# Eight early dense groups in place of nine, with the ninth's first steps kept in DRAM during the experts

## The reference

```python
# A: state space block and dense FFN, in sequences of 512 tokens
u  = rmsnorm(xn, ssm_norm_w)
Bu = einsum('btd,nd->btn', u, B_w)            # 64 states
h_t = sigmoid(log_lambda) * h_(t-1) + Bu_t    # a scan along the 512 tokens
x1 = xn + einsum('btn,dn->btd', hs, C_w) + D_skip * u
z  = rmsnorm(x1, ffn_norm_w)
A  = x1 + (silu(z @ w1.T) * (z @ w3.T)) @ w2.T          # inner size 688
# M: mixture of 32 experts, 8 per token, and a shared expert
scores = sigmoid(xn @ gate_w.T)               # best 4 of 8 groups, then the best 8 experts
routed = sum over the 8 of weight * (silu(xn @ w_gate[e].T) * (xn @ w_up[e].T)) @ w_down[e].T
shared = (silu(xn @ sh_gate.T) * (xn @ sh_up.T)) @ sh_down.T
```

## Time and profile before

| | us |
|---|---|
| median of 3 runs | 1865.17 (1863.17 to 1865.59) |
| the profiled execution | 1864.31 |
| its span | 1862.4 |
| PE busy in it (matmuls) | 1764.0 (95%) |
| DVE busy | 949.2 (51%) |
| ACT busy | 627.5 (34%) |
| POOL busy | 1033.7 (56%) |

### The profile page before, as it was taken

How to read it: one execution, slowest core, us unless ns; L and a number is a source line. 1 busy time by engine, 2 the same in 40 slices (tenths; PEclk the granted TensorE clock), 3 DMA queues, 4 the chain that set the end, 5 groups by cost and what they waited for, 6 DMA issues and landing times.

```text
span 1862.4 us, 27141 instructions
## 1 busy us (share of the span) xinstructions
PE 1764.0 (95%) x8166; PEld 1323.1 (71%) x8168; DVE 949.2 (51%) x2464; ACT 627.5 (34%) x1349; POOL 1033.7 (56%) x1058
## 2 busy tenths in 40 slices
PE   5798899999989999999999999999999969999995
PEld 2455565666658888888888888888888846666653
DVE  6577556433314444444444555556556535555555
ACT  5621222222214444444444444444444322222220
POOL 0001777777777777771000665555556067777776
PEclk9898999999989999999999999999999979999997
DMA  6714333645478899986555898889898554333333
GB/s 208 248 45 136 135 128 142 216 157 221 151 280 275 290 289 292 287 287 205 172 176 170 257 281 268 272 267 276 265 277 265 180 163 117 113 114 103 103 105 105
DMA packets 262594, 374.29 MB, mean 201 GB/s; under 512 B 30916, under 2 KB 227640, under 8 KB 261688
## 3 DMA queue, kind: packets, MB, share of 16 engines
q1 hardware_dynamic: 212392, 227.51, 39.4%
q0 software_dynamic: 49920, 145.03, 23.4%
q10 hardware_dynamic: 144, 0.03, 0.0%
HBM read 189.47 MB, written 182.98 MB: 200 GB/s over the span
## 4 chain that ended last, share of the span: by engine, by line
PE 89%; DVE 6%; DMA 1%; issue 1%; ACT 1%; POOL 1%; SPq 1%; POOLq 0%; DVEq 0%; ACTq 0%
PE ps L1260 27%; PE ps L1178 19%; PE ps L1277 13%; PE ps L1195 11%; PE ps L1251 7%; PE ps L1270 3%; PE ps L1160 2%; PE ps L1131 2%; PE ps L1098 1%; PE ps L1147 1%; PE ps L1170 1%; DMA big<-in_x 1%; POOL xe L529 1%; PE ps L1091 1%; SPq L366 0%
## 5 line engine op out<-in xcount | busy, mean ns | idle before, releaser
L529 POOL DMA_INDIRECT xe<-results,slots x512 | 517.5, 1011 | 490.8 <-DMA results<-arena 232.8
L1260 PE MATMUL ps<-big,arena 128*128 x2304 | 546.4, 380 | 2.2 <-ACT arena L647 2.2
L1260 PEld LDWEIGHTS ps<-big,arena 128*128 128x128 f32 x2304 | 427.9, 190 | 73.5 <-issue 3.0
L1028 DVE SCALAR_TENSOR_TENSOR arena<-arena,ps 128x128 f32<-128x128 f32 x576 | 175.0, 344 | 467.3 <-ACT arena L652 393.6
L518 POOL DMA_INDIRECT sorted_rows<-big,slots x256 | 258.3, 1009 | 84.0 <-issue 77.8
L1277 PE MATMUL ps<-big,arena 128*128 x1152 | 296.2, 380 | 0.0
L518 POOL DMA_INDIRECT sorted_rows<-xe,slots x256 | 246.3, 962 | 78.1 <-issue 78.1
L1178 PE MATMUL ps<-arena,w 128*128 128x512 f32 x640 | 287.7, 592 | 0.0
L620 ACT ACTIVATE arena<-ps 128x512 f32<-128x512 f32 (+1 forms) x128 | 76.3, 596 | 544.4 <-PE ps L1178 500.5
L937 DVE TENSOR_TENSOR arena<-arena,ps 128x512 f32<-128x512 f32 (+1 forms) x128 | 88.0, 688 | 329.3 <-ACT arena L620 328.1
L652 ACT ACTIVATE arena<-ps 128x256 f32<-128x256 f32 x288 | 110.7, 384 | 390.9 <-PE ps L1260 390.9
(11 more groups left out here) (160 smaller groups left out, 1355.6 us busy)
## 6 DMA issues: line engine op xcount, KB each, us to landing
arena<-sorted_rows SPq DMA_DIRECT2D x288, 288.0 KB, 3.9
results<-arena SPq DMA_DIRECT2D x288, 256.0 KB, 3.8
big<-in_x SPq DMA_DIRECT2D x32, 512.0 KB, 4.3
sorted_rows<-big SPq DMA_DIRECT2D x2, 4608.0 KB, 23.8
xe<-results,slots POOLq DMA_INDIRECT x512
out<-xe SPq DMA_DIRECT2D x64, 128.0 KB, 2.5
sorted_rows<-big SPq DMA_DIRECT2D x48, 144.0 KB, 1.8
big<-in_wexp SPq DMA_DIRECT2D x1, 5632.0 KB, 20.1
```

The costliest lines, as they stand in the source:

```text
L529: pool.indirect_dma_start(out=gathered_at[i % RING][:, k, :], out_offset=None, in_=results[half], in_offset=bass.IndirectOffsetOnAxis(ap=s ...
L1028: last = nc.vector.scalar_tensor_tensor(eh[n % 2][:, s, :], eg[n % 2][:, s, :], rows[n % RING][:, s, ds(e + D, 1)], ps[:, 2 + n % 2, (2 * ...
L1260: last = mm(ps[:, 2 + n % 2, s * D:(s + 1) * D], rT[n % 2][:, (2 * s + c) * P:(2 * s + c + 1) * P], big[:, ds(at_w + 2 * c * INNER, 2 * IN ...
```

## The change

There are eight early groups, 0 to 7 (`FIRST` = 8), and eight late ones, 8 to 15. The first steps of group 8 are still made inside group 7, and what they leave is kept in DRAM while the experts use the arena: `xT` in `kept_xT`, `zT` in `kept_zT`, and the sum of x and x1 in the rows of `parts`. After the experts the three are loaded again, and group 8 starts from them; the separate first steps in front of the late groups are gone. x is loaded anew for groups 9 to 15 (the four input tiles for 9 to 12 at once). There are eight places for gathered tiles in half 1 (four of them in `big`, over the expert weights), and four as before in half 0. In the last group the four last tiles are combined ahead of the wait for the last down product, and the down products are then added from PSUM to each tile.

```diff
     UP_AT = 64
-    FIRST = 9
+    FIRST = HT // GT
     LATE = range(FIRST, GROUPS)
...
         xe = sb("xe", [P, HT * ROW])
         rows_of = [big[:, AT_ROWS:].rearrange("p (t w) -> p t w", w=ROW), xe[:, :].rearrange("p (t w) -> p t w", w=ROW)]
-        gathered_at = [xe[:, j * K * D:(j + 1) * K * D].rearrange("p (k d) -> p k d", d=D) for j in range(RING)]
+
+        DEEP = 2 * RING
+        gathered_at = [a.rearrange("p (k d) -> p k d", d=D) for a in
+                       [xe[:, j * K * D:(j + 1) * K * D] for j in range(RING)]
+                       + [big[:, AT_ROWS + j * K * D:AT_ROWS + (j + 1) * K * D] for j in range(DEEP - RING)]]
+
+        def place(i):
+
+            return i % RING if i < HT else i % DEEP
+
+        def turn(i):
+
+            return i // RING if i < HT else (i - HT) // DEEP + (HT // RING if i % DEEP < RING else 0)
         part_tile = [xe[:, (RING * K + j) * D:(RING * K + j + 1) * D] for j in range(RING)]
...
             for g in range(FIRST - 1):
-                if g + 4 < FIRST:
+                if g + 4 <= FIRST:
                     sp.wait_ge(x_used, g + 1)
                     load_x(g + 4, g + 4)
...
                     load_wexp(0, AT_X)
             sp.wait_ge(x_used, FIRST)
-            load_wexp(AT_X, AT_ROWS)
             sp.wait_ge(xposed, FIRST)
             for j in range(4):
                 sp.wait_ge(scattered[0][j], 16 * K * QUARTER)
                 load_wexp(AT_ROWS + j * QUARTER * ROW, AT_ROWS + (j + 1) * QUARTER * ROW)
-            store_part(FIRST - 1)
+            sp.wait_ge(xT_ready, FIRST + 1)
+            sp.dma_start(kept_xT, xT.rearrange("p c n -> p (c n)")).then_inc(xT_stored, 16)
+            sp.wait_ge(x_used, FIRST + 1)
+            load_wexp(AT_X, AT_ROWS)
+            sp.dma_start(group_rows(parts, FIRST), part_early[FIRST % 2]).then_inc(part_kept, 16)
 
 
             def load_rows(n):
...
                 sp.wait_ge(summed, i + 1)
-                sp.dma_start(out[i * P:(i + 1) * P, :], gathered_at[i % RING][:, 0, :]).then_inc(out_stored[i % RING], 16)
-
-            sp.wait_ge(zposed, FIRST)
-            sp.wait_ge(gu_ready, CH * (FIRST - 1) + 2)
-            sp.wait_ge(rms_z_ready, FIRST)
+                sp.dma_start(out[i * P:(i + 1) * P, :], gathered_at[place(i)][:, 0, :]).then_inc(out_stored[place(i)], 16)
+
+            sp.wait_ge(xT_stored, 16)
+            sp.wait_ge(y_ready, FIRST + 1)
+            sp.wait_ge(z_ready, FIRST + 1)
             for n in range(RING):
                 load_rows(n)
+            sp.wait_ge(zT_ready, FIRST + 1)
+            sp.dma_start(kept_zT, zT.rearrange("p c n -> p (c n)")).then_inc(zT_stored, 16)
+            store_part(FIRST - 1)
             for par in range(2):
                 sp.wait_ge(part_stored[par], 16 * len(range(par, FIRST, 2)))
             for m in range(ALL + 2):
@@ -451,6 +478,8 @@
                         scattered_all(sp, 1)
                     if m + RING < ALL:
                         load_rows(m + RING)
+                    if m == ALL - 3:
+                        sp.dma_start(xT.rearrange("p c n -> p (c n)"), kept_xT).then_inc(xT_reloaded, 16)
                 n = m - 2
                 if n < 0:
...
             assert not summed_after(ALL - 2) and not summed_after(ALL - 1)
 
-            for g in range(FIRST, FIRST + 4):
+            for q in range(2):
+                sp.wait_ge(ey_stored[q], 16 * (ALL // RING))
+            sp.wait_ge(zT_stored, 16)
+            sp.dma_start(zT.rearrange("p c n -> p (c n)"), kept_zT).then_inc(zT_reloaded, 16)
+            for g in range(FIRST + 1, FIRST + 5):
                 load_x(g, g)
-            for i in range(HT, HT + GT):
-                load_part(i)
+            sp.wait_ge(part_kept, 16)
+            sp.dma_start(part_of(FIRST), group_rows(parts, FIRST)).then_inc(part_reloaded, 16)
             for g in LATE:
                 for t in range(GT):
-                    store_out((g - 1) * GT + t)
-                    if t == 2 and g + 4 < GROUPS:
-                        sp.wait_ge(x_used, g + 1)
-                        load_x(g + 4, g + 4)
+                    if g > FIRST:
+                        store_out((g - 1) * GT + t)
+                    if t == 2 and g + 5 < GROUPS:
+                        sp.wait_ge(x_used, g + 2)
+                        load_x(g + 5, g + 5)
             for t in range(GT):
                 store_out((GROUPS - 1) * GT + t)
-            for q in range(RING):
-                sp.wait_ge(out_stored[q], 16 * (NT // RING))
+            for i in range(NT - DEEP, NT):
+                sp.wait_ge(out_stored[place(i)], 16 * (turn(i) + 1))
 
 
...
+                    if turn(i):
+                        pool.wait_ge(out_stored[place(i)], 16 * turn(i))
                     for k in range(K):
                         pool.indirect_dma_start(
-                            out=gathered_at[i % RING][:, k, :], out_offset=None, in_=results[half],
+                            out=gathered_at[place(i)][:, k, :], out_offset=None, in_=results[half],
                             in_offset=bass.IndirectOffsetOnAxis(ap=slots[:, i, k:k + 1], axis=0)
-                        ).then_inc(gathered[i % RING], 16)
+                        ).then_inc(gathered[place(i)], 16)
 
 
         @block.scalar
...
             for g in range(FIRST):
-                act_group(g, g + 1 < FIRST)
+                act_group(g, True)
 
...
 
                 act.wait_ge(ey_ready, n + 1)
+                if n == 0:
+                    act.wait_ge(zT_stored, 16)
                 if n >= RING:
                     act.wait_ge(ey_stored[n % RING], 16 * (n // RING))
...
             e_out(ALL - 1)
 
-            act.wait_ge(ey_dve, ALL)
-            xT_copy(FIRST)
-            results_stored(act, ALL)
-            rms_z(FIRST)
-            zT_copy(FIRST)
             for g in LATE:
                 act_group(g, g + 1 < GROUPS)
...
                 dve.wait_ge(x_loaded[n % 4], 16 * ((GROUPS + n) // 4 + 1))
-                if 2 <= n < FIRST:
+                if 2 <= n <= FIRST:
                     dve.wait_ge(part_stored[n % 2], 16 * (n // 2))
-                tt(part_of(n), x_of(n), x1, ALU.add).then_inc(x_used, 1)
+                tt(part_early[n % 2] if n == FIRST else part_of(n), x_of(n), x1, ALU.add).then_inc(x_used, 1)
 
             def make_z(n):
...
             def finish_part(g):
                 dve.wait_ge(down_done, CH * (g + 1))
+                if g == FIRST:
+                    dve.wait_ge(part_reloaded, 16)
                 for b in range(2):
                     last = tt(part_of(g)[:, 2 * b:2 * b + 2, :], part_of(g)[:, 2 * b:2 * b + 2, :],
...
                     dve.wait_ge(part_loaded[i % RING], 16 * (i // RING + 1))
                     rest = part_tile[i % RING]
-                tt(y[:, 0, :], y[:, 0, :], rest, ALU.add).then_inc(summed, 1)
+                last = tt(y[:, 0, :], y[:, 0, :], rest, ALU.add)
+                if i // GT < GROUPS - 1:
+                    last.then_inc(summed, 1)
+                else:
+                    do(last)
 
             def combine(i):
                 for j in range(SUMS):
                     sum_step(i, j)
+
+            def finish_tiles():
+
+                tiles = range((GROUPS - 1) * GT, NT)
+                for i in tiles:
+                    combine(i)
+                dve.wait_ge(down_done, CH * GROUPS)
+                for t, i in enumerate(tiles):
+                    tt(gathered_at[place(i)][:, 0, :], gathered_at[place(i)][:, 0, :],
+                       ps[:, 6 + t // 2, t % 2 * D:(t % 2 + 1) * D], ALU.add).then_inc(summed, 1)
 
             def dve_group(g, more):
...
                     if g < FIRST:
                         route(g, s)
-                    elif s % 2 == 1:
+                    elif s % 2 == 1 and g > FIRST:
                         combine((g - 1) * GT + s // 2)
                     if more and s == 2:
                         bu_scale(g + 1)
@@ -982,7 +1029,10 @@
                         make_x1(g + 1)
                     if more and s == 6:
                         make_z(g + 1)
-                finish_part(g)
+                if g < GROUPS - 1:
+                    finish_part(g)
+                else:
+                    finish_tiles()
                 if g < FIRST:
                     route_late(g)
...
             e_out(ALL - 1)
 
-            dve.wait_ge(ey_act, ALL)
-            a1_norm(FIRST)
-            bu_scale(FIRST)
-            scan(FIRST)
-            make_x1(FIRST)
-            make_z(FIRST)
             results_stored(dve, ALL)
             for g in LATE:
                 dve_group(g, g + 1 < GROUPS)
-            for t in range(GT):
-                combine((GROUPS - 1) * GT + t)
 
 
...
                         pe.wait_ge(zT_ready, g + 1)
+                        if g == FIRST:
+                            pe.wait_ge(zT_reloaded, 16)
                     gu_product(g, s)
                     if more and s == 1:
...
 
```

(44 more changed lines are left out.)

## The result

The changed kernel takes 1877.47 us (median of 4 runs, 1876.14 to 1879.22), the kernel before 1865.0: a ratio of 1.0069, 95% interval 1.0052 to 1.0087, or 12.5 us slower. The forecast was 1881, 16 slower, with a range of 1874 to 1888. The profiled execution took 1877.15 us, its span is 1875.5; the span before was 1862.4, so 13.1 us are to be found in the trace.

A forecast was written before the change was run, and what follows sets the result against it. TensorE (PE), busy 95% of the span, was taken as the bound. Terms +4.1 - 26.9 + 45.9 - 7.0 = +16.1 us on the profiled 1864.3 gave 1880.4; with 0.9 for the median, 1881, range 1874 to 1888.

The forecast's parts named there:

- The start of the experts: Between early groups and experts: last scatter, then SP's queue, put the first expert product at 555.0 for 550.92, +4.1 us.
- the sum: Adding queue times after the last scatter lands at 524.4: last part lands at 554.1, first expert product at 555.0.
- 2176 KB (two parts and the rows) at 190: In SP's queue before the experts: two parts and four pairs' rows load or store at 190 GB/s, 11.7 us.
- the fixed 1.6 us: In SP's queue before the experts: a fixed time added once to the transfer times, read from weight loads' landing times.
- The first 3712 KB, at 264 GB/s: In SP's queue after the last scatter: last weight quarter, xT and the weights at `AT_X` take 14.4 us.
- all bytes at 264 GB/s give 551.7 or +0.8: Bound for the first expert product if SP's whole queue drains at 264 GB/s: 551.7, +0.8 us.
- The rival of an earlier start: Scatters do not hold the experts: first expert product at 510.5, -40.4 us, time 1836 to 1837; chance 0.03.
- The rival of a faster queue: SP's queue drains at the fabric's rate: first expert product at 542.4, -8.5 us, time 1868.7; chance 0.05.
- The later one: Scatter lands late, parts and rows drain below 190 GB/s, group 9's x comes late: up to 1890; chance 0.10.
- The boundary: From experts to late groups: the gap falls from 28.7 to 1.8 us, 1.2 of it waiting for group 9's x; -26.9 us.
- The late groups: After the experts: eight groups instead of seven take 365.7 us in place of 319.9, +45.9 us.
- The tail: From PE's end to the span's: eight places remove the gather wait, 22.8 us falls to 15.8, -7.0 us.

The follow-up runs named there:

- the further scatters: 16 further indirect DMAs on POOL ahead of half 0's last quarter of scatters: in the changed kernel 1904.29 us, in the kernel before 1872.42 us.
- its order: Changed kernel with SP's stores and loads that don't need the last scatters put ahead of the wait for them: 1860.03 us, ratio 0.9976 to the kernel before.
- holding the scatters: Changed kernel with POOL's scatters of half 1 held until all early parts are stored: 1869.68 us, ratio 1.0032 to the kernel before.
- nine groups with kept steps: Changed kernel with nine early groups again, group 9's first steps made inside group 8 and kept in DRAM: 1846.17 us, ratio 0.9903 to the kernel before.
- the wait for the parts left out: Kernel with nine early groups and kept steps, without ACT's and DVE's wait for the stored parts before the first pair: 1841.8 us, ratio 0.9877 to the kernel before.
- without the wait for the parts: Changed kernel without ACT's and DVE's wait for the stored parts before the first pair: 1872.95 us, ratio 1.0044 to the kernel before.

## Why the prediction was right, and where it was off

**The start of the experts** decided it, as forecast. The last scatter's issue (523.21, forecast 521.8) is what all hangs on, shown by the further scatters: the same insertion is paid in full after the change and by a third to a half before it. The queue behind it was the second part, shown by its order (17.7 us). The landing of the last scatter came 1.3 us later than the sum had it (525.67, forecast 524.4). From there to the first product it took 26.6 us; the sum said 30.6.

The step that was mis-sized is "2176 KB (two parts and the rows) at 190", with the fixed 1.6 us beside it. The first 3712 KB, at 264 GB/s, came out nearly as reckoned: the weights at `AT_X`, the last of them, landed at 540.4, 14.8 us after the first issue, where 14.4 and the fixed 1.6 make 16.0. What was left, the two parts, the rows and zT, landed 11.0 us later (551.4), where the sum had 13.7; in that stretch the queue moved 245 GB/s. I had taken the 190 from the 9 us at the start of the experts before. The same view by queue shows what it is: in these 9 us SP's queue moved 1.70 MB, which is all that stood in it (1664 KB). So 190 is a mean over a short queue with its beginning and its end, and the fixed 1.6 us were added to a rate that held a start already. In the middle, from 546 to 550, that queue moved 225 GB/s; why not 245 was not tried. The reading behind the 1.6 is weak too: the 2048 KB load of 9.4 us was not alone, three more loads were issued within 2 us behind it. The bound "all bytes at 264 GB/s give 551.7 or +0.8" is the nearest to what was measured.

That scatters and queue share one capacity, as the sum assumed, is shown by holding the scatters: 20.2 us. The Trainium skill's fit ("DMA: Bandwidth & Descriptors", section "Anatomy of one DMA") is stated for a single DMA issued from GpSimd, while these are ten on SP's queue. An estimate by it, 17 us for these bytes, is 2.3 below what the lone queue took from its first issue to the landing of its last part (19.3), and far from the shared queue (25.7).

**The rival of an earlier start** is refuted: PE waited for the scatters, and a delay of 26.7 us at them was one of 26.6 at its start. **The rival of a faster queue** was right in its direction and not in its size: the queue was faster than the sum had it, but the first product came at +1.4, not -8.5. **The later one** did not come.

**The boundary** went as worked out: the reload of xT and zT cost nothing visible, and x of group 9 came 0.44 us late, not 1.2. **The late groups** took 46.1 us more, against 45.9. **The tail** gave 6.2 of 7.0. DVE's last addition ended 13.55 us after PE, as reckoned (13.6): the tiles followed one another at 2.90 us after the first and not at 2.83, the four additions from PSUM took 1.42 and not 1.7. What was missed is the store behind it, 3.0 us (1872.45 to 1875.5) in place of 2.24; the four last stores are issued one behind another there, in 1.80 us, where before only one was left. That the gain comes from the places, as I argued, is shown. That they would be enough in any arrangement would have been wrong, since POOL's own pace is the next bound (nine groups with kept steps).

So the change holds two gains, 27.6 us at the boundary and 6.2 in the tail, and pays for them with a group moved from a place where it covered a wait to a place where it covers nothing: 46.1 us and a start not a microsecond earlier. Without that price, with nine early groups, the gain at the boundary stays whole, but the one in the tail doesn't: POOL's gathers then set the end, and 18.6 us are gained, or 23 with the wait for the parts left out.

## What to carry to other kernels

Before moving work away from a stretch, ask what else is running beneath it to a fixed end: a wait that the chain doesn't name, because an engine is busy over it, is found in the other engines' timelines (here POOL's last scatter at 521.8, long before PE was free). An in-order queue lengthens such a wait (here by 17.7 us): what doesn't depend on the late event belongs ahead of it. And a buffer that lets one engine run ahead pays only until that engine's own pace is the limit.

## What the runs showed of the hardware that I had not expected

The 16 DMA engines moved about 400 GB/s in all over 10 us and more, with packets of 1 KB and 1152 B among them, both with POOL's scatters beside SP's queue (397 and 398) and with the queue alone (407). Two streams at once got no more out of them than one.

SP took longer to issue the same DMAs in one case: the four loads of rows took 5.6 us to issue in the changed kernel (534.58 to 540.16) and 2.7 in the kernel before, where little stood ahead of them in the queue. The queue's length alone doesn't do it: with the scatters held it was as long, and the four took 2.72 us (from 531.59). Only a long queue and the scatters together gave 5.2 to 5.6 (5.18 without the wait for the parts, 5.59 with the further scatters); why is not shown.

After more than 40 us without work PE's clock was at 0.50, the lower level of 1.2 GHz, as after 6 us before; the first product took 3.5 us now and 3.8 before, where one takes 1.9 later.
